# Decoder block in one kernel: the order of TensorE's work inside a key tile of the self-attention loop

## The reference

```python
q, k, v = proj(Wq, bq), proj(Wk, bk), proj(Wv, bv)        # 16 heads of 16
attn = einsum('bhld,bhrd->bhlr', q, k) * scale
dist = clip(arange(L)[None, :] - arange(L)[:, None], -64, 8) + 64
rel  = einsum('bhld,lrd->bhlr', q, dist_emb[dist]) * scale
out  = softmax(attn + rel) @ v                            # then @ Wo.T + bo
```

## Time and profile before

| | |
|---|---|
| median of 3 runs | 1477.4 us (1474.54 to 1479.12) |
| profiled execution | 1474.41 us |
| its span | 1472.6 us |
| the self-attention loop | 158 to 993 us, 835 us |
| PE busy over the span | 1287.8 us, 87% |
| DVE, ACT, POOL busy | 1066.9, 940.4, 337.0 us |

### The profile page before, as it was taken

One profiled execution on the slowest core, in us unless ns is written; L12 is line 12 of the kernel. 1 busy time (PEld: TensorE's weight loads), 2 busy tenths in 40 slices (PEclk: granted clock), 3 DMA queues, 4 the chain that ended last, 5 costly groups with the idle time before them and its releaser, 6 DMA issues. The chain is left out here.

```text
span 1472.6 us, 24890 instructions
## 1 busy us (share of the span) xinstructions
PE 1287.8 (87%) x8220; PEld 686.6 (47%) x8220; DVE 1066.9 (72%) x2589; ACT 940.4 (64%) x1650; POOL 337.0 (23%) x577
## 2 busy tenths in 40 slices
PE   8695899999999999999999999999995998810597
PEld 4342343344344334334434434437884787600486
DVE  4466778888877887887887888762663568999655
ACT  3331677777777777777777777773674559749600
POOL 3342112121121211212112121004552005600012
PEclk9897999999999999999999999999997999965799
DMA  8999886977877878788697786615411003316032
GB/s 246 275 296 263 224 213 196 262 210 207 238 203 233 217 218 225 206 247 209 198 257 211 214 227 181 199 73 168 115 58 44 1 1 129 135 51 228 0 111 90
DMA packets 260303, 260.55 MB, mean 177 GB/s; under 512 B 65838, under 2 KB 246606, under 8 KB 256078
## 3 DMA queue, kind: packets, MB, share of 16 engines
q1 hardware_dynamic: 260174, 258.95, 61.0%
HBM read 147.40 MB, written 110.71 MB: 175 GB/s over the span
## 5 line engine op out<-in xcount | busy, mean ns | idle before, releaser
L556 ACT ACTIVATE pr<-scoresT 128x512 f32<-128x512 f32 x1024 | 550.5, 600 | 217.9 <-PE scoresT L816 159.3
L812 PE MATMUL scoresT<-qT,kT 99*128 99x512 bf16 (+7 forms) x1408 | 359.0, 326 | 7.1 <-DMA qT<-sh 5.4
L659 DVE TENSOR_REDUCE mx<-scores_for_max 128x1 f32<-128x888 f32 (+6 forms) x448 | 301.5, 673 | 0.1
L654 DVE CUSTOM_DVE_ANT_0 junk<-scores_for_max,win 128x200 f32<-128x200 f32 (+2 forms) x512 | 179.9, 351 | 162.1 <-PE scores_for_max L787 154.5
L657 DVE TENSOR_REDUCE mx<-scores_for_max 128x1 f32<-128x64 f32 (+6 forms) x448 | 277.4, 619 | 0.1
L812 PEld LDWEIGHTS scoresT<-qT,kT 99*128 99x128 bf16 (+1 forms) x1408 | 113.6, 97 | 335.2 <-ACT rows L536 97.8
L829 PE MATMUL attn_out<-pr,vS 128*17 128x512 f32 x2048 | 269.5, 598 | 0.1
L816 PE MATMUL scoresT<-idf,win 128*128 128x128 f32 x1024 | 218.4, 274 | 0.0
L449 POOL COPY rows<-rows 128x736 f32<-128x736 f32 x128 | 102.1, 798 | 399.5 <-ACT rows L536 399.5
L786 PE MATMUL scores_for_max<-kX,qT 64*128 64x512 bf16 x512 | 165.7, 386 | 10.7 <-DVE mx L659 9.4
L787 PE MATMUL scores_for_max<-kX,qX 64*128 64x512 bf16 x512 | 165.6, 385 | 0.0
(11 more groups left out here) (204 smaller groups left out, 1778.0 us busy)
## 6 DMA issues: line engine op xcount, KB each, us to landing
rel_table<-rows SPq DMA_DIRECT2D x128, 512.0 KB, 4.5
win<-rel_table SPq DMA_DIRECT2D x128, 512.0 KB, 5.4
up_raw<-xT_normed SPq DMA_DIRECT2D x6, 1536.0 KB, 5.0
xT_normed<-up_raw SPq DMA_DIRECT2D x6, 1536.0 KB, 7.3
qT<-q_parts SPq DMA_DIRECT2D x32, 256.0 KB, 7.6
kX<-k_parts SPq DMA_DIRECT2D x64, 128.0 KB, 4.8
kT<-k_parts SPq DMA_DIRECT2D x32, 256.0 KB, 5.4
q_parts<-shared SPq DMA_DIRECT2D x32, 192.0 KB, 5.2
```

Source lines behind the costliest of these rows:

```text
L556: nc.scalar.activation(pr[:, n % NPR, h, :], bank, ACT.Exp).then_inc(t_read, 1)
L654: last = nc.vector.tensor_tensor_reduce(junk[:, n % 2, 0:z - a], bank[:, a:z], win[:, T % NW, q4, h, u:u + z - a], 1.0, NEG, ALU.add, ALU. ...
L659: last = nc.vector.tensor_reduce(mx[:, T % 2, q4, h, 2:3], bank[:, z:L], AX.X, ALU.max)
L812: last = mm(bank[:, a:e], k[0:r], q[0:r, a:e], start=(n == 0), stop=not near and n == len(pieces) - 1, skip_group_check=True)
```

## The change

In a period PE makes the weighted sums of the key tile before straight after the three scores, and then the two pairs for the maxima, the fourth score and the small product. ACT copies the finished sums of `T - 1` after the four exponentials of kt = 0 and ahead of the row of that period, no longer between the first and the second exponential of kt = 1. The list `order`, the ring of banks, the semaphores and the counts of all instructions stay.

```diff
@@ ACT @@
                 for kt in range(TL):
                     for h in range(G):
                         exps(T, kt, h)
-                        if kt == 1 and h == 0 and T:
-                            copy_out(T - 1)
+                    if kt == 0 and T:
+                        copy_out(T - 1)
                     if kt in ROW_AT and T + 3 < NT:
                         copy_row(T + 3, ROW_AT[kt])
@@ PE @@
                 for kt in range(TL):
                     for h in range(G - 1):
                         scores(T, kt, h)
+                    if kt:
+                        weigh(T, kt - 1)
+                    elif T:
+                        weigh(T - 1, TL - 1)
                     for c in chunks_of(T, kt):
                         max_chunk(*c)
                     scores(T, kt, G - 1)
...
                     if kt == SHIFT_AT and T + 1 < NT:
                         turn_shift(T + 1)
-                    if kt:
-                        weigh(T, kt - 1)
-                    elif T:
-                        weigh(T - 1, TL - 1)
             weigh(NT - 1, TL - 1)
             turn_out(NT - 1)
```

## The result

| | median | profiled execution | span |
|---|---|---|---|
| before | 1477.79 us (4 runs) | 1474.41 us | 1472.6 us |
| after | 1525.12 us (1521.24 to 1525.68, 4 runs) | 1524.85 us | 1523.1 us |

The ratio is 1.0318, with a 95% interval of 1.0294 to 1.0342. The changed kernel is 47 us slower by the medians and 50.5 us by the spans. 1545 was forecast, with a range of 1500 to 1585.

What follows compares the result with a forecast made beforehand. PE was taken to bound the loop, with ACT's answer joining its path: 4.70 us more per pair of T over 14.5 pairs is 68, plus 1 for the last three T; 1474.4 + 69 = 1543.4, so 1545 us, range 1500 to 1585.

Steps and rivals of the forecast that it cites:

- The mechanism: With weigh ahead of the pairs and s3, ACT's reads come onto PE's path: 1545 us, chance 0.73.
- the sum: Lengths of 16 periods over an even and an odd T: 57.59 us per pair, 4.70 more than before.
- the second s: Second of two score costs in a period's length, both taken at that period's own cost, about 0.22 to 0.45 us.
- s': Cost of one score of the following period, about 0.22 to 0.45 us by its near tiles.
- The list of waits of before: Profile before: 97.8 us of scores waiting for row reads, claimed to be the weight loader's, not PE's own.
- the rival "no change": If the 97.8 us were true PE waits, moving weigh would change nothing: 1477 us, chance 0.04.
- The step from weigh to the pairs: PE going from weigh to the first max pair: 0.99 us start to start, including a step of 0.12.
- the hidden and the double step: Rivals on weigh to pairs: step costs nothing, 28 us less, 1517, chance 0.10; or double, 28 more, 1573, chance 0.08.
- The release of a bank: From the end of ACT's read to the PE product waiting for that bank: 0.15 us in each period.
- The last three T: End of the loop, without rows and later without pairs: 1 us added, with 0 and 3 as ends.
- The copy: ACT's copy of finished sums, moved ahead of kt = 0's row: costs 0.49 us, against about 0.8 if left.
- The rival "faster": One change of form less per period with ACT's answer hidden: 23 us less in all, 1454 us, chance 0.05.

Runs made afterwards that it cites:

- the edits of ACT's answer: Small ScalarE copy added, or fourth head's exponential done at half width: on the changed kernel 1536.83 and 1484.55 us, on the kernel before 1477.91 and 1476.59.

## Why the prediction was right

- *The mechanism.* Right. In 232 of 256 periods a score now waits on PE for ACT, and the edits of ACT's answer move the time after and not before. Nor do errors cancel in the sum: from weigh to weigh each of its 16 periods measures 0.07 to 0.11 us less than it says, once the second s is taken as the s' of the next period.
- *The list of waits of before was PEld's.* Right. Had the 97.8 us been waits of PE, the half-width exponential in the kernel before would have found them; by its starts PE waits 3 us between scores there. With that the rival "no change" falls.
- *The step from weigh to the pairs*, the unknown one: taken at 0.99 from start to start, measured 618.44 - 617.45 = 0.99. It is 0.98 or 0.99 in all 243 places of the loop. Both rivals on it, the hidden and the double step, fall. The prediction read one thing wrongly here: the Trainium skill ("TensorE: Matmul & The Clock Gate", "The mechanism") lets a weight load be pulled ahead when it goes to a row group that is not in use, and weigh has 128 contraction rows (`128*17` in its rows), which leave none free for the pairs; so that half of the rule gave no reason for a hidden step. The other half, a load into the background buffer, did not show either: the load of the first pair starts at 618.43, 0.01 us before the pair.
- *The release of a bank.* This is the term that was mis-sized: 0.05 us and not 0.15, since the forecast read it at a product with two waits. Every period of the sum holds it once, and 0.10 x 16 = 1.6 us per pair turn 57.59 into 55.99, against 56.11 measured. Over 14.5 pairs it is 23 us, where 20 lie between 1545 and 1525.
- *The last three T*, taken at 1 us, came to 1.7. *DVE* stayed hidden: its waits for pairs in the loop grew from 145.6 to 195.9 us.
- *The copy.* Too large: with weigh moved, its new place saves 4 us of the loop over the old one, where some 0.3 us for each T, 10 us, had been reckoned.
- *The rival "faster".* The change of form that it counted on is saved, 20 us of the loop, but against 68 us of new waits. Its condition, exponentials of half the length, was tried on the fourth head alone: 1484.55 us, still above before.
- *What was to be seen.* Kt = 0 of even T is the longest period, as forecast. The waits between scores are 96 us in all where 100 to 120 had been named, and 0.58 us in the period shown, where the sum had 0.69; most of the difference is the release again.

## What to carry to other kernels

Where two engines hand banks of a short ring to each other, follow the ring once round and write down what stands between the consumer's last read and the producer's next write: work placed there hides the answer, and when the same work is moved ahead of the last write, PE waits for whatever part of the answer nothing else covers. Busy shares did not show it: by its records PE was 98% busy in the loop before and still 95% after, ACT 75% and 69%, and 0.2 us of ACT's answer in a period was worth 41 us in one order and nothing in the other. When a move leaves a remainder, look for the in-order engine on which an unrelated step stands in front (here the reciprocals), and before delaying a step ask for the transfer that comes after it.

## What the runs showed of the hardware

- From the end of a ScalarE read to the matmul that waits for its bank 0.05 us pass where the program gives the matmul one semaphore wait, and 0.14 where it gives it two, though the second was met long before.
- A ScalarE copy of 128 x 1 has a record of 0.19 us but delays what follows by 0.09.
- Weigh (32-column tiles) straight to the pairs (64-row tiles) costs as much as weigh to a full-array score: 0.99 us from start to start in both.
- Records of matmuls hide short waits: PE's busy time in the loop leaves 882.0 - 834.5 = 48 us idle after the change, while its starts show 99 us of waits.
